# A fused transformer layer on one core: the rows of negated maxima are sent from ScalarE's DMA queue instead of SyncE's

## What is computed

```
x = x + attn_a(layernorm(x))                       # 32 heads of 8, window 128
x = x + ffn(layernorm(x))                          # relu, 256 -> 1024 -> 256
x = x + attn_b(layernorm(x))                       # convolution, delta scan, gated MLP
x = x + ffn(layernorm(x))
...
# attn_a: queries of block i see keys of blocks i-1 and i
scores = q . k / sqrt(8); probs = softmax(scores); out = probs . v
```

## Time and profile before

| What | us |
|---|---|
| median of three runs (range) | 1532.42 (1528.03 to 1537.56) |
| the profiled execution | 1531.66 |
| its span, first to last instruction | 1529.9 |
| PE busy in matmuls | 1123.7 (73%) |
| DVE busy | 927.0 (61%) |
| ACT busy | 504.9 (33%) |
| POOL (GpSimd) busy | 174.2 (11%) |

### The profile page before, as it was taken

How to read it: one execution, slowest core, us unless ns; L and a number is a source line. 1 busy time by engine, 2 the same in 40 slices (tenths; PEclk the granted TensorE clock), 3 DMA queues, 4 the chain that set the end, 5 groups by cost and what they waited for, 6 DMA issues and landing times.

```text
span 1529.9 us, 22243 instructions
## 1 busy us (share of the span) xinstructions
PE 1123.7 (73%) x8586; PEld 744.0 (49%) x8600; DVE 927.0 (61%) x2425; ACT 504.9 (33%) x1043; POOL 174.2 (11%) x251
## 2 busy tenths in 40 slices
PE   5487748687878788787878787878878787676037
PEld 3154515364646555455645554556546554454025
DVE  3613367683758566683768476864768476637831
ACT  1042334234432434224432434334422533242011
POOL 2000000300021000401030000300030003001300
PEclk9588868788979799788988799889988898779559
DMA  9425023401241023401241024201241021001000
GB/s 292 56 39 48 5 68 45 42 22 55 31 54 18 22 69 49 38 22 55 31 54 17 22 69 58 29 22 55 44 48 17 21 64 9 1 14 62 0 14 7
DMA packets 112490, 64.57 MB, mean 42 GB/s; under 512 B 49473, under 2 KB 106753, under 8 KB 112385
## 3 DMA queue, kind: packets, MB, share of 16 engines
q1 hardware_dynamic: 109328, 58.01, 21.9%
q10 hardware_dynamic: 3056, 5.15, 1.1%
HBM read 45.55 MB, written 17.17 MB: 41 GB/s over the span
## 4 chain that ended last, share of the span: by engine, by line
PE 50%; DVE 19%; DMA 11%; SPq 10%; ACT 6%; issue 5%; POOL 1%; DVEq 0%; ACTq 0%; POOLq 0%
PE bank L1624 6%; PE bank L1373 5%; PE bank L1365 5%; PE bank L1475 5%; PE bank L1549 5%; DMA k_stack<-k_pieces 4%; DMA q_stack<-m_rows 4%; DVE conv L1006 4%; PE bank L1647 4%; PE bank L1455 3%; PE bank L1426 3%; PE bank L1345 3%; SPq L369 2%; PE bank L1460 2%; SPq L367 2%
## 5 line engine op out<-in xcount | busy, mean ns | idle before, releaser
L675 ACT ACTIVATE probs<-bank 128x512 f32<-128x512 f32 x256 | 152.0, 597 | 301.9 <-PE bank L1460 301.4
L935 DVE TENSOR_REDUCE mx<-bank 128x2 f32<-128x320 f32 x256 | 121.3, 487 | 152.3 <-PE bank L1426 146.9
L1475 PE MATMUL bank<-probs,v_ext 128*9 128x128 f32 x2048 | 169.5, 288 | 21.4 <-ACT probs L675 16.2
L1421 PE MATMUL bank<-edge_mask,identb 128*128 128x64 bf16 x512 | 62.9, 208 | 121.2 <-DMA k_stack<-k_pieces 82.9
L334 POOL TENSOR_TENSOR lane_buf<-state,q_l 128x128 f32<-128x128 f32 x128 | 86.0, 701 | 401.9 <-DVEq L1138 401.9
L1177 DVE TENSOR_TENSOR hid_c<-bank,probs 128x256 f32<-128x256 f32 (+1 forms) x48 | 19.6, 421 | 163.3 <-ACT probs L792 99.4
L1421 PEld LDWEIGHTS bank<-edge_mask,identb 128*128 128x128 bf16 x512 | 32.7, 100 | 174.5 <-DMA k_stack<-k_pieces 93.4
L1475 PEld LDWEIGHTS bank<-probs,v_ext 128*9 128x9 f32 x2048 | 85.1, 93 | 63.8 <-issue 19.2
L1455 PE MATMUL bank<-tri_mask,identb 128*128 128x512 bf16 x256 | 107.1, 418 | 11.3 <-DMA q_stack<-m_rows 10.6
L1113 DVE TENSOR_TENSOR lane_buf<-state,til 128x128 f32<-128x128 f32 x256 | 102.7, 401 | 18.0 <-POOL lane_buf L559 10.1
L1460 PE MATMUL bank<-q_stack,k_stack 128*128 128x128 bf16 x1024 | 106.7, 231 | 0.0
(11 more groups left out here) (158 smaller groups left out, 1791.0 us busy)
## 6 DMA issues: line engine op xcount, KB each, us to landing
k_stack<-k_pieces SPq DMA_DIRECT2D x192, 64.0 KB
q_stack<-q_pieces SPq DMA_DIRECT2D x192, 32.0 KB
q_l<-lane_q SPq DMA_DIRECT2D x8, 512.0 KB, 4.0
k_l<-lane_k SPq DMA_DIRECT2D x8, 512.0 KB, 4.7
q_pieces<-conv SPq DMA_DIRECT2D x24, 128.0 KB, 2.1
k_pieces<-conv SPq DMA_DIRECT2D x48, 64.0 KB, 2.0
hid<-in_x SPq DMA_DIRECT2D x8, 256.0 KB, 2.8
x_in<-in_x SPq DMA_DIRECT2D x8, 256.0 KB, 2.9
```

Of the source, the lines that this page charges most:

```text
L675: act.activation(probs[:, u % 2], score_bank[u % 2][:], ACT.Exp, scale=float(DK) ** -0.5).then_inc(exp_done, 1)
L935: dve.tensor_reduce(mx[:, g, 2 * v:2 * v + 2], bank[1 + u % 2][:, 0:2 * SPAN].rearrange("p (h k) -> p h k", h=2), AX.X, ALU.max).then_inc( ...
L1421: pe.matmul(edges[:, :, e * W:e * W + SUB], identb[:], edge_mask[:, e * SUB:(e + 1) * SUB].rearrange("p (o s) -> p o s", o=1) .broadcast_t ...
L1475: last = pe.matmul(bank[5][row:row + VE, col:col + W], v_ext[:, b, kb, h, :], probs[:, u % 2, (hp * 2 + kb) * W:(hp * 2 + kb + 1) * W], st ...
```

## The change

`load_max` is removed from SP's program with all its calls. In its place `max_rows` on ACT waits for its own copy and issues the same three DMAs, on ACT's DMA queue. The semaphores, the data and the tiles are the same. 32 groups (4 in each of 8 blocks) have three DMAs each, so 96 DMAs move.

```
-            def load_max(n, g):
-
-                sp.wait_ge(m_copied, n * NG + g + 1)
-                for j in range(3):
-                    sp.dma_start(q_stack[MROW + j:MROW + j + 1, slot(n, g)], m_rows[j * HPH:(j + 1) * HPH, g % 2, :]
-                                 ).then_inc(m_in[slot(n, g)], 16)
...
                     next_stacks(t + 2, 0)
-                if following:
-                    load_max(n, 3)
                 if front:
                     next_stacks(t + 2, 1)
                     next_stacks(t + 2, 2)
-                    load_max(t + 2, 0)
-                    load_max(t + 2, 1)
                 if scan:
                     outputs_out(t)
                     outputs_in(t)
                 if front:
-                    load_max(t + 2, 2)
                     load_residual(t + 2)
...
             load_x(1)
-            for g in range(DONE_EARLY):
-                load_max(0, g)
             body(-1, scan=False)
...
                 act.copy(m_rows[:, g % 2], max_bank[0:3 * HPH, 0:W]).then_inc(m_copied, 1)
+                act.wait_ge(m_copied, n * NG + g + 1)
+                for j in range(3):
+                    act.dma_start(q_stack[MROW + j:MROW + j + 1, slot(n, g)], m_rows[j * HPH:(j + 1) * HPH, g % 2, :]
+                                  ).then_inc(m_in[slot(n, g)], 16)
```

## The result

The changed kernel takes 1550.94 us in the median of four runs (1547.55 to 1555.14), the kernel before 1531.34 us beside it (1528.03 to 1537.56). The ratio is 1.0125 with a 95% interval of 1.0081 to 1.0168: 1.25% slower, some 19 us (12 to 26). The forecast was 1538.5 us with a range up to 1547. The direction was right and the size was not: the time fell outside the range, where I had put one chance in ten.

A forecast was written before the change was run, and what follows sets the result against it. No engine is full; the chain runs 50% over PE, 19% DVE, 21% transfers and SP's queue. -5.7 + 1 + 4.9 + 1.6 + 3.0 + 2.0 = +6.8 us on 1531.66 gives 1538.5 us, range 1527 to 1547.

The forecast's parts named there:

- the price of a triple: On ACT's queue: issuing three DMAs holds ACT 1.8 us, taken from the same DMAs on SP.
- cheap issues: Rival, chance 0.15: ACT spends 0.3 us per DMA, 0.9 a triple, and the gain stands; 1527 us.
- group 2: Behind group 2's copy on ACT: output norm 0.5 us later in six blocks, +3.0 us.
- the start: Ahead of block 0: three groups' triples on ACT delay the first exponential, +2.0 us.
- the covers: Unit 22 of blocks 0 to 6 (8 us to spare) and group 0 (1.6 us): ACT's delay is hidden, 0.
- the wait of block 7: At block 7's unit 22: SP had issued at once, so PE's 2.96 us wait stays; 0.
- the first term: Unit 24, blocks 0 to 6: rows issued earlier from ACT land before PE needs them, -5.7 us.
- the second rival: No earlier landing, chance 0.12: rows still land behind stack 0, costs stay, gain goes; 1543 us.
- group 1: Behind group 1's copy on ACT: norm applied late, +4.9 us in blocks 1 to 6, +1.6 in block 0.
- slowed issues: Rival, chance 0.1: ACT's issues at groups 0 and 1 take 1.2 us each while stack 2 streams; 1554 us.
- all of it is on the path: Group 1's late norm: PE's turn of `tok` and the first net wait behind it, so 0.8 us counts fully.
- the clock: Chance 0.03 for a better outcome by TensorE's clock falling differently (0.836 granted on average).

The follow-up runs named there:

- group 2 alone: Kernel before with only group 2's rows (blocks 1 to 7) issued from ACT, the rest on SP: 1.0013 [0.9987, 1.0039], +2 us.
- that group alone: Kernel before with only group 3's rows (units 22 to 24) issued from ACT, the rest on SP: 1.0027 [1.0002, 1.0052], +4 us.
- Group 1 alone: Kernel before with only group 1's rows (blocks 1 to 7) issued from ACT, the rest on SP: 1.0111 [1.0078, 1.0143], +17 us.
- three copies: Kernel before, DMAs still on SP, plus three unread copies on ACT behind group 1's copy: 1.0108 [1.0076, 1.0140], +16.5 us.
- kernels without a late norm: Six variants delaying the norm by 0.6 us at most: group 3 alone, group 2 alone, one copy, later issues, one DMA from either queue; 0.9931 to 1.0027.
- the row of doses: Kernel before plus one, two, three, four or six unread copies on ACT behind group 1's copy: 0, +5.7, +16.5, +15.2, +25.4 us.
- four copies: Kernel before, DMAs still on SP, plus four unread copies on ACT behind group 1's copy: 1.0099 [1.0061, 1.0137], +15.2 us.
- the one DMA: One DMA of 48 rows per group instead of three: changed kernel (ACT) 0.9942, kernel before (SP) 0.9931, both against the kernel before.
- six copies: Kernel before, DMAs still on SP, plus six unread copies on ACT behind group 1's copy: 1.0166 [1.0135, 1.0197], +25.4 us.

## Why the prediction was right or wrong

**Right: the price of a triple.** 1.8 us was forecast from SP's rows; the median issue on ACT is 608 ns, the triples mostly 1.79 to 1.83 us. The cases of cheap issues fell with it.

**Right: group 2, the start, and the covers.** +0.5 in six blocks is what the profile shows and what the kernel with group 2 alone bears out (+2 us, interval -2 to +6); the start has +2.2 for 2.0. Unit 22 and group 0 are covered, and the wait of block 7 stays, 3.5 us.

**Wrong: the first term, -5.7 at unit 24.** The step that failed is "if they need not stand behind stack 0's packets". I had noted that no row of before shows it, and then took the whole gain and gave it 0.6. Measured are 1.6 us of gain between the copies in the profile, and none in the kernel with that group alone. In block 3 the last of three landed 9.9 us after its issue from ACT, 9.7 from SP. By the Trainium skill (DMA: Bandwidth & Descriptors, "Queues, rings and completion order") the DMA engines take turns between the queues, which pointed to the gain. The same section of the Trainium skill says that the semaphore's write lands only behind the earlier writes of that DMA engine, whichever queue they came by, which points against it. The trace has room for both. Half of the rows' packets were started 5.0 to 8.4 us late although they stood in ACT's queue, so taking turns did not bring them past the stack, and their updates came some 2.5 us behind the packets, where the early half's came 0.3 to 0.8 us behind. The rule of the Trainium skill that stood under the second rival (same page, "Issuing engines are not separate DMA queues"), that issuing from several engines saves only the sequencer's time, is the one that held.

**Mis-sized: group 1.** 6.5 us forecast, 8.3 in the profile, since in three blocks the triple took up to 0.6 us longer. That is a small part of what "slowed issues" meant. This rival had nearly the right time, 1554, by the wrong way: it wanted 1.0 us per issue and more, and the median was 0.61. It rested on a row of SP's queue, 1.19 us, read as an issue into a full queue; that a queue was full no row shows.

**Missing, and the largest error: what a late norm costs beyond its delay.** I had said "all of it is on the path" and left it at one us for one, 6.5 us for group 1. Group 1 alone made 17 us with 7.4 directly late, and three copies in its place 16.5 with 6.6. That a late norm can cost such an extra is measured; what the extra consists of is not shown. The granted clock at the scan's projections was low in three of the seven blocks of the changed kernel and in all seven with three copies, and the time there 5.6 and 9.3 us longer than before. But kernels without a late norm have 2.4 to 4.2 us of that too. The forecast gave the clock 0.03, and only as a gain. With what the profile shows put in, 1.6 of gain, 15.2 from group 1's copy to group 2's, 3.0 and 2.2, the sum is +18.8, 1550.5 us. That is bookkeeping after the fact from a single profile, and no proof.

**What stays open.** Where the extra comes from; the row of doses has it at 0, 3.5, 10, 4 and 5 us with ±5 each. For the whole change it is 7 us, 19 less the 12 that stand at the places of the edit, with ±7. Why products elsewhere in time get less of the upper clock, and with it whether some other delay of the same size would have been free: four copies cost no more than three. And what holds half of a triple's rows, and all of the one DMA's, behind the stack on another queue.

## What to carry to other kernels

Before a DMA is issued from a compute engine, look at what stands behind it in that engine's order and how long that can wait: here 1.8 us against a slack of 0.7 cost 17 us, the same issues two instructions later cost nothing that could be told, and the busy share of the engine (33%) said nothing about either. Merge small DMAs of one source first, whichever engine issues them; it saved issue time, and after the issue the rows were down 1.4 to 3.7 us sooner from ACT and 0.1 to 3.0 from SP. And a delay can cost more than its length: here 16 to 17 us for 7 in two kernels, and a quarter to a third more than its length with four and six copies. Put that into the range.

## What was not expected of the hardware

- Of three small DMAs issued together behind some 590 KB on SP's queue, half of the 48 rows were down after 3.4 us and the other half only after 7.7 to 11.1, when ACT issued them; after 3.3, and 9.5 to 11.0, when SP did (block 3). Another issuing engine is no faster lane.
- One DMA of 48 rows to three partitions takes 0.72 us to issue from ACT and 0.78 from SP, three of 16 rows 1.8. It too landed behind the stack, 5.6 to 9.5 us after its issue, and was still on time at all seven unit 24s, from either queue.
- Eight products a block that nobody reads made the kernel 9 us faster and five others 14, both at places where PE had waited. With the eight the granted clock over the first net behind them went from 0.78 to 0.94. With the five it went, ahead of group 2's copy, from 0.72 to 0.86 in four blocks and 1.00 in two.
- The same part of the kernel ran at different granted clocks from one profile to the next. From the first of the scan's projections to group 2's copy the seven blocks took 37.7 us before and 40.1 to 41.9 in six kernels of about the same or a shorter time. A difference of a few us there, between two single profiles, can't be laid to an edit.
